# A two-layer vision transformer on one core: the V weight's and the embedding weight's way into memory at the start, the order of work at the beginning of each half of heads, and the router's place

## The reference

```python
def reference(x, ...):
    h = tok(x)                  # patches @ W_lin.T + b_lin, class token in front, + positions
    h = h + attn0(norm(h))      # 16 heads of 64; softmax(q k' / 8), causal mask, @ wo.T
    h = h + ffn0(norm(h))       # 256 -> 1024 -> 256, rounded to 1/256; gelu by 33 knots
    h = h + attn1(norm(h))      # 16 heads of 64, no mask, + bo
    return h + moe(norm(h))

def moe(x):                     # 8 experts, each 256 -> 1024 -> 256, all computed for all tokens
    logits = einsum('bld,ed->ble', x, gate_weight)
    kth = sort(logits.reshape(-1))[4 * 256 * 6 - 1]     # one threshold over all logits
    gates = logits * (logits >= kth)
    hh = gelu(einsum('bld,ehd->bleh', x, w1) + b1)
    y = einsum('bleh,edh->blde', hh, w2) + b2.T
    return einsum('blde,ble->bld', y, gates)
```

## Time and profile before

| what | value |
| --- | --- |
| median of three executions | 1000.7 us |
| the profiled execution's own time | 1000.7 us |
| its span | 998.9 us |
| TensorE, VectorE, ScalarE, GpSimd busy | 941.7, 579.5, 544.4, 154.6 us |
| 0 to 55 us (opening, first scores): TensorE busy | 41.19 us |
| 55 to 230 us (most of layer 0's attention): TensorE busy | 168.69 of 175 us |
| 230 to 345 us (its end, feed-forward): TensorE busy | 103.81 of 115 us |
| 355 to 528 us (most of layer 1's attention): TensorE busy | 166.60 of 173 us |
| 528 to 575 us (expert stage's start): TensorE busy | 37.35 of 47 us |
| 575 to 998.9 us (experts): TensorE busy | 414.60 of 423.9 us |

### The profile page before, as it was taken

The page is one execution under the profiler, slowest core; times in us unless marked ns, Lnnn a source line. Parts: engine busy times, 40 slices in busy tenths (PEclk is TensorE's granted clock), DMA queues, the critical chain, the costliest instruction groups (busy, mean ns, idle before and its releaser), DMA issues.

```text
span 998.9 us, 18661 instructions
## 1 busy us (share of the span) xinstructions
PE 941.7 (94%) x7159; PEld 870.7 (87%) x7159; DVE 579.5 (58%) x1251; ACT 544.4 (54%) x1570; POOL 154.6 (15%) x173
## 2 busy tenths in 40 slices
PE   5899999999799999999996899999999999999998
PEld 5877888888677878888886898999999999999998
DVE  5466574747899574666664486655354544544342
ACT  4466465643764664646554453756464756555452
POOL 0142122211000121222210000151011111101111
PEclk9999999999999999999999799999999999999999
DMA  7320000002000210000011011101111111100001
GB/s 277 136 76 1 1 2 2 2 1 84 3 1 1 85 43 2 1 2 1 1 43 43 1 62 67 43 1 43 43 44 43 43 43 44 43 1 1 1 14 37
DMA packets 8653, 34.48 MB, mean 35 GB/s; under 512 B 626, under 2 KB 5106, under 8 KB 5236
## 3 DMA queue, kind: packets, MB, share of 16 engines
q1 hardware_dynamic: 8564, 33.28, 9.2%
HBM read 32.06 MB, written 1.22 MB: 33 GB/s over the span
## 4 chain that ended last, share of the span: by engine, by line
issue 31%; PE 24%; POOL 5%; DVE 5%; ACT 2%; POOLq 0%; DVEq 0%; ACTq 0%
PE D L553 8%; PE O L553 7%; POOL h L348 4%; PE O L694 2%; PE T L680 2%; PE S L669 1%; DVE wslot L1094 1%; PE S L553 1%; DVE hid L1481 1%; PE S L663 1%; POOL h L360 1%; ACT hid L1066 1%; ACT work L1062 1%; PE O L799 1%; POOL vbuf L358 1%
## 5 line engine op out<-in xcount | busy, mean ns | idle before, releaser
L1481 DVE TENSOR_TENSOR hid<-work,hid 128x300 fp32r<-128x300 f32 (+1 forms) x256 | 139.3, 564 | 200.1 <-ACT hid L1066 200.0
L553 PE MATMUL O<-hid,wslot 128*128 128x300 f32 (+3 forms) x1680 | 242.4, 302 | 0.0
L553 PEld LDWEIGHTS O<-hid,wslot 128*128 128x128 f32 x1680 | 234.7, 190 | 0.6
L553 PE MATMUL D<-xn,wslot 128*128 128x300 f32 (+3 forms) x1368 | 224.4, 309 | 4.6 <-ACT work L950 2.6
L553 PEld LDWEIGHTS D<-xn,wslot 128*128 128x128 f32 x1368 | 198.8, 190 | 10.0 <-ACT work L950 2.9
L1062 ACT ACTIVATE work<-D,prm 128x300 f32<-128x300 f32 (+1 forms) x128 | 66.7, 521 | 185.6 <-PE D L553 185.5
L960 ACT ACTIVATE probs<-S,negmax 111x111 f32<-111x111 f32 (+1 forms) x352 | 117.5, 359 | 53.4 <-DVE negmax L1242 53.2
L532 POOL TENSOR_TENSOR probs<-probs,rsum 111x444 f32<-111x444 f32 (+1 forms) x88 | 80.9, 920 | 379.8 <-DVE rsum L1250 379.8
L553 PE MATMUL S<-xn,wslot 128*128 128x300 f32 (+3 forms) x864 | 137.1, 306 | 0.0
L553 PEld LDWEIGHTS S<-xn,wslot 128*128 128x128 f32 x864 | 126.4, 193 | 0.3
L1242 DVE TENSOR_REDUCE negmax<-S 111x4 f32<-111x444 f32 (+1 forms) x88 | 52.6, 600 | 72.1 <-PE S L669 72.1
(11 more groups left out here) (163 smaller groups left out, 1158.7 us busy)
## 6 DMA issues: line engine op xcount, KB each, us to landing
raw<-in_moe SPq DMA_DIRECT2D x16, 1024.0 KB, 4.8
raw<-in_attn SPq DMA_DIRECT2D x8, 1024.0 KB, 4.9
work<-in_x SPq DMA_DIRECT2D x2, 1008.0 KB, 7.9
raw<-in_ffn SPq DMA_DIRECT2D x1, 1024.0 KB, 4.7
w2f<-in_ffn SPq DMA_DIRECT2D x1, 1024.0 KB, 6.8
raw<-in_x SPq DMA_DIRECT2D x2, 504.0 KB, 5.5
out<-h SPq DMA_DIRECT2D x3, 300.0 KB, 2.7
raw<-in_w_lin SPq DMA_DIRECT2D x1, 768.0 KB, 4.1
```

The lines of the kernel that those rows point to most:

```text
L553: mm = pe.matmul(psum, a, b, start=(first and k == 0), stop=(k == 3 * n - 1))
L1481: nc.vector.tensor_tensor(moe_hid(s, 1), moe_g(s)[:, 0:w], moe_hid(s, 0).bitcast(F32), ALU.subtract).then_inc(m_hid, 1)
```

## The change

1. The raw transfer of V's weight of layer 0 goes into `w2f` and waits for nothing. The second feed-forward weight, which lands in `w2f` too, waits for V's split. The other pieces close ranks in the two raw buffers (`RING`). GpSimd's split of V waits for K's low part.
2. The embedding weight is transferred and split in two halves, interleaved with the halves of chunk 0 of x. TensorE multiplies both output halves with the first half of the rows, then both with the second.
3. The masks are cast between the two drains of chunk 1. The twelve idle matmuls go.
4. In the first round of a half the transposes of u-1 come before the scores of u on TensorE, and their copy before the row maximum on VectorE. At u = 0 the V product comes before the scores.
5. The router's chunks 0 to 2 and the last mean move to the end of `attention(1)`, into banks of their own, the last variance behind s = 0, the last normalisation ahead of the experts on ScalarE and VectorE. The last two quarters of the first expert's second weight are split behind it. Chunk 3 of the router follows s = 5. The search starts after s = 5 in place of s = 8. `gateT` is cleared whole in layer 1's fifth round, and no longer at the start of the search.

```diff
+        RING = [0, 1] + [i for i in range(FIRST_W, NPIECE) if i not in (V_ATTN0, W2_FF)]
@@ sync
+                if i == V_ATTN0:
+                    sp.dma_start(w2f[:, :], weights[i - FIRST_W]).then_inc(v0_in, 16)
+                    continue
                 if i == W2_FF:
+                    sp.wait_ge(*piece_split(V_ATTN0))
                     sp.dma_start(w2f[:, :], weights[i - FIRST_W]).then_inc(w2_in, 16)
                     continue
+                if i >= FIRST_W:
+                    sp.wait_ge(*piece_split(RING[ring(i) - 2]))
+                if i == 0:
+                    sp.dma_start(w_half(dst, 0), w_half(src, 0)).then_inc(w_in, 16)
+                    dst, src = w_half(dst, 1), w_half(src, 1)
@@ gpsimd, split
+                if i == V_ATTN0:
+                    pool.wait_ge(*piece_split(i - 1))
@@ tensor, router
+            ROUTER_BANK = [BO[0], BT[0], BS[1], BO[1]]
+            def turn_logits(c):
+                pe.wait_ge(lt_out, max(c, 1) + 1)
@@ tensor, attention
                 for i in range(8):
-                    if l == 0 and i == QH:
-                        keep_busy("qk", i, 12)
                     project_qk(i)
...
-                    if u < NUNIT:
+                    if half_begins(u):
+                        if u == 0:
+                            project_v(u)
+                        else:
+                            transposes(2 * u - 2)
                         scores(u)
-                    if 0 <= u - 1 < NUNIT:
-                        transposes(2 * u - 2)
-                    if u < NUNIT:
+                    else:
+                        if u < NUNIT:
+                            scores(u)
+                        if 0 <= u - 1 < NUNIT:
+                            transposes(2 * u - 2)
+                    if 0 < u < NUNIT:
                         project_v(u)
...
                         values(u - 1)
+                    if l == 1 and u == NUNIT + 1:
+                        router(0)
                     if due is not None:
                         project_out(due, 1)
+                    if l == 1 and u == NUNIT + 1:
+                        router(1)
+                        mean(3, 3)
+                        router(2)
@@ tensor, start
+            pe.wait_ge(w_low, 1)
+            pe.wait_ge(x0_low, 1)
+            for dc in range(KD):
+                embed_part(0, dc, range(KF // 2), True, False)
             pe.wait_ge(*piece_split(0))
-            embed(0, 0)
-            embed(0, 1)
+            pe.wait_ge(*piece_split(1))
+            for dc in range(KD):
+                embed_part(0, dc, range(KF // 2, KF), False, True)
@@ tensor, moe_up
-                    if s == 1:
-                        mean(3, 3)
-                    if s == 4:
+                    if s == 0:
                         variance(3, 3)
-                    if s in (2, 3, 5):
-                        router((2, 3, 5).index(s))
-                    if s in (5, 6, 7):
-                        turn_logits(s - 5)
-                    if s == KH:
+                    if s in (2, 3, 4):
+                        turn_logits(s - 2)
+                    if s == 5:
+                        router(3)
+                    if s == 6:
                         turn_logits(3)
@@ scalar
             square(3, 3)
+            inv_root(3, 3)
...
-                if s == 6:
-                    nc.scalar.preload_act_table_set("natural_log_exp_and_others")
-                    inv_root(3, 3)
@@ vector, prepare_gates
-                nc.vector.memset(gateR.bitcast(F32), 0.0).then_inc(params, 1)
+                nc.vector.memset(gateT[:, :].bitcast(F32), 0.0).then_inc(params, 1)
@@ vector, experts
+            finish(3, 3)
+            for k in (SPLITS - 2, SPLITS - 1):
+                low_quarter(FIRST_W + W_MOE + 1, k)
...
+                if s == 2:
+                    move_logits(3)
                 if s == 5:
-                    finish(3, 3)
-                if 4 <= s <= 7:
-                    move_logits(s - 4)
-                if s == KH:
                     start_search()
-                if m % 2 == 0 and 1 <= n <= 4:
+                if s == 6:
+                    search(0)
+                if m % 2 == 0 and 1 <= n <= 4 and s > KH:
                     search(8 * (n - 1) + m // 2)
```

More of the change, by code:

```diff
@@ L242, in ring @@
         def ring(i):
-            return i if i < 2 else i - 3 - past(i)
+            return RING.index(i)
         def piece_split(i):
@@ L412, in place_in_half, with half_begins @@
             return GROUPS[c].index(g), len(GROUPS[c])
+        def half_begins(u):
+            return u < NUNIT and place_in_half(u)[0] == 0
         def qk_blocks(u):
@@ L565, in normed, with embed_part @@
                 return [xn[:, k, kk, sl] for k in range(2)]
+            def embed_part(c, dc, ks, first, last):
+                a, w = CHUNKS[c]
+                wl = [wslot[:, WSLOTS - 1, k, 0:KF * D].rearrange("p (a n) -> p a n", n=D) for k in range(2)]
+                for i in ks:
+                    (wh, ww) = [t[:, i, dc * P:(dc + 1) * P] for t in wl]
+                    (xh, xl) = [hid[:, c % 2, k, i * w:(i + 1) * w] for k in range(2)]
+                    for a, b in ((wh, xh), (wh, xl), (ww, xh)):
+                        mm = pe.matmul(BD[dc][:, 0:w], a, b, start=first, stop=(last and i == KF - 1 and a is ww))
+                        first = False
+                if last:
+                    mm.then_inc(emb_mm, 1)
             def embed(c, dc):
-                a, w = CHUNKS[c]
                 if dc == 0:
[L571 to L579, removed]
+                    pe.wait_ge(*piece_split(1 + c))
+                pe.wait_ge(h_set, KD * (c - 1) + dc + 1)
+                embed_part(c, dc, range(KF), True, True)
             NORMED = [h_set, h_attn[0], h_ff, h_attn[1]]
@@ L611, in variance, with router @@
                 mm.then_inc(ln_var[n], 1)
+            ROUTER_BANK = [BO[0], BT[0], BS[1], BO[1]]
+            def router(c):
+                a, w = CHUNKS[c]
+                if c == 0:
+                    pe.wait_ge(params, 6)
+                pe.wait_ge(ln_out[3], c + 1)
+                split_products(pe, ROUTER_BANK[c][0:GROWS, 0:w],
+                               lambda i: [gateR[:, k, i, :] for k in range(2)],
+                               lambda i: normed(i, slice(a, a + w)), KD, lt_mm)
+            def turn_logits(c):
+                pe.wait_ge(lt_out, max(c, 1) + 1)
+                for g in GROUPS[c]:
+                    mm = pe.transpose(BT[0][0:NTOK[g], g * E:(g + 1) * E], logT[0:E, cols(g)], ident[0:E, 0:E])
+                mm.then_inc(log_mm, 1)
             def attention(l, n):
@@ L807, in _ @@
             attention(1, 2)
[L809 to L826, removed]
             def sum_counts(i):
@@ L1095, in low_quarter, with build_masks @@
                                         ALU.subtract).then_inc(dve_split if k == SPLITS - 1 else dve_part, 1)
+            def build_masks():
+                dve.wait_ge(mats_in, 64)
+                nc.vector.tensor_copy(masku[:, :], maskf[:, 2, :]).then_inc(masks, 1)
+                for l in range(2):
+                    for i in range(QH):
+                        ins = nc.vector.tensor_copy(maskb[:, l, i, :], maskf[:, l, :])
+                ins.then_inc(masks, 1)
             def set_h(c):
                 for dc in range(KD):
+                    if c == 1 and dc == 1:
+                        build_masks()
                     dve.wait_ge(emb_mm, KD * c + dc + 1)
@@ L1162, in low_x0, with low_w @@
                                         ALU.subtract).then_inc(start_split if k else x0_low, 1)
-            low_part(0)
+            def low_w(k):
+                dve.wait_ge(*((high_ready, 1) if k else (w_high, 1)))
+                high, low = piece_place(0)
+                nc.vector.tensor_tensor(w_half(low, k), w_half(piece_raw(0), k), w_half(high.bitcast(F32), k),
+                                        ALU.subtract).then_inc(start_split if k else w_low, 1)
+            low_w(0)
             low_x0(0)
+            low_w(1)
             low_x0(1)
@@ L1178, in _ @@
             low_part(2)
-            dve.wait_ge(mats_in, 64)
-            nc.vector.tensor_copy(masku[:, :], maskf[:, 2, :]).then_inc(masks, 1)
-            for l in range(2):
-                for i in range(QH):
-                    ins = nc.vector.tensor_copy(maskb[:, l, i, :], maskf[:, l, :])
-            ins.then_inc(masks, 1)
             dve.wait_ge(params, 3)
@@ L1289, in attention @@
                     due = out_due(u)
-                    if u < NUNIT:
+                    if half_begins(u):
+                        if u > 0:
+                            move_t(2 * u - 2)
                         row_max(2 * u)
-                    if 0 <= u - 1 < NUNIT:
-                        move_t(2 * u - 2)
+                    else:
+                        if u < NUNIT:
+                            row_max(2 * u)
```

(4 more changed lines are left out.)

43 lines of the change are left out of this document (26 added, 17 removed).

## The result

The changed kernel took 984.56 us (median of four; 982.26 to 987.36) against 1000.82 before. The ratio is 0.9846, interval [0.9815, 0.9877]: about 15 us faster, 16.3 by the medians. The forecast was 24.5 us faster, 976.2 us, in a range that ended at 984.5. The profiled execution took 987.36 us, with a span of 985.6 against 998.9.

The account below looks back on a forecast made before the run. TensorE, busy 94% of the span, was taken to bound the kernel. Gains of 6.3 + 6.0 + 12.2 = 24.5 us from 1000.7 gave 976.2 us, range 969.5 to 984.5.

Parts of the forecast that it names:

- Part 1: The opening: earlier first start, masks moved, V's weight without a wait; first transposes at 50.35, gain 6.3 us (4 to 7.3).
- Part 2: Half beginnings: transposes fill the wait before the scores, 0.41 us at each of 14; net gain 6.0 us (3 to 7.7).
- covered by 0.7 us: Half beginnings: a row maximum 0.53 us late ends the last exponential at 76.8, before the next scores start at 77.5.
- the 1.2 us for second transposes: Half beginnings: second transposes that waited for VectorE's copy, three of eight places, wait less; a gain of 1.2 us.
- The term of 0.45 us for layer 1's first unit: Layer 1's first unit: scores come later behind the V product, so the next scores begin 0.45 us later, a loss.
- Rival B: Opening and half beginnings: GpSimd sets the first transposes, late row maxima the next scores; low ends give 981.5 us, chance 0.16.
- the signs named for being wrong: Scores at half beginnings still wait, second scores of halves wait for exponentials, or a new stand opens before the fifth group.
- Rival D: Attention: clock closes, with fillers gone and new stands of 1.3 and 0.5 us before the first transposes; 1006 us, chance 0.03.
- Rival A: Expert stage: no second clock drop behind the second count's stand, 2.4 us less, so 973.8 us; chance 0.32.
- after 9 us at full rate: Expert stage: argument against no second clock drop, that the same stand closed the gate before, after 9 us at full rate.
- Part 3: The expert stage's start: router and normalisation work moved earlier, first count at 544.3 instead of 556.30; gain 12.2 us (9 to 13).

Follow-up runs that it names:

- old beginnings: The change with scores first again, on both engines, at all half beginnings but layer 0's first: 980.23 us, ratio 0.9792 to the kernel before.
- TensorE's new order alone: The change with VectorE's old order at half beginnings (row maximum before the copy of the first transposes), TensorE's new order kept: 978.39 us, ratio 0.9777.
- the copy first: The change with VectorE's copy of the second transposes ahead of the first reciprocal at half beginnings: 975.30 us, ratio 0.9746 to the kernel before.
- the best version: The copy first, plus layer 1's first unit in the old order and ScalarE's two expert weight copies moved behind the 16th group: 972.42 us, ratio 0.9716.

## Why the prediction was wrong

- **Part 1, +6.3 forecast, +6.2 measured.** The path was right: GpSimd ended last. V's split took 4.83 us for 4.55, which was absorbed: the output weight's copy followed the last Q/K copy and not V's split. The embedding gave 0.6 us less than written. That shift reached the first projection (34.94 for 34.4) and shrank on the way only because the forecast had sized the later steps a little long: the output weight's copy came at 43.01 for 42.7, the transposes at 50.48 for 50.35. And other profiles of the same opening gain 5.1 to 6.5 us. So the path was right, and the agreement within 0.1 us was luck.
- **Part 2, +6.0 forecast: the step that failed.** "Put ahead of the scores they fill the wait: scores start as before, and what is behind them comes 0.41 us earlier." The scores did start so. But what is behind them did not come 0.41 us earlier. The row maximum's 0.53 us was followed only to the next scores ("covered by 0.7 us"), not to the values. Values need a copy that VectorE issues behind a reciprocal, and so behind the first exponentials. Without clock falls part 2 came to -5.3 + 3.1 = -2.2 us. The experiments show it. Where VectorE comes late out of a normalisation, its old order brings the values back to 5.19 us after the scores, the kernel before's own figure, so even without the swap the 0.41 us is not gained there. The copy ahead of the reciprocal brings them to 4.54. Over the fourteen beginnings (from layer 0's third and layer 1's second score group to each layer's last) the lead fell by 1.5 us in the change (clock taken out), stayed with the old beginnings, grew by 2.6 with TensorE's new order alone, and by 5.8 with the copy first; forecast were 6.5 before the loss at layer 1's first unit. One term was also too large: of the 1.2 us for second transposes some 0.75 came with the copy first, for at three beginnings the lead grew by 0.63 us instead of 0.38. The term of 0.45 us for layer 1's first unit held: the lead went from 5.42 to 4.96.
- **Rival B** had seen that late row maxima could eat the gain, but with the next scores as the ones that wait, and with 3 us left of part 2 at the least. None of the signs named for being wrong came at the fourteen beginnings: scores wait at most 0.2 us there, the only scores that wait for exponentials are the two of the layers' second units, and no stand opened before the expert stage's fifth group. The wait that did come, at the values, had no sign in the forecast.
- **The clock.** Rival D named lapses in the attention, but for lost fillers and at the first transposes. They came behind the new stands, in some executions: 3.1 us in each of two profiles, and 1.5 us more in one of them. Part 2's stands were not foreseen, so neither were these. Rival A asked for no fall behind the second count; in this profile it came (12 matmuls in 3.35 us), in those of the new order on TensorE alone and of the copy first it did not, with the same stand of 2.21 us. The forecast's reading that the gate had closed before "after 9 us at full rate" is off: in the kernel before full rate had lasted from 555.5 to 562.3, 6.8 us, with the stand inside.
- **Part 3, +12.2 forecast, +12.3 measured.** The forecast's own terms give a first count at 544.25, so 12.05 us and not 12.2; that changes nothing. The half rate from 545 to 556 us in the kernel before is in this gain: the forecast took its paces per group at full rate, so it had this gain in its sum without naming it. TensorE worked there from 546.1 to 555.5; at full rate half of that would have done, so by this estimate some 4.7 of the 12.3 us are clock. The stand of 2.2 us stayed, as written. That it hung on ScalarE's weight copies is shown by the best version.

With -2.2 for +6.0 and one fall of 3.1 us the forecast's own sum is 976.2 + 8.2 + 3.1 = 987.5; the profiled execution took 987.36. This closes the account and proves nothing more, for the -2.2 and the 3.1 are read from that same execution.

## What to carry to other kernels

When an operation is swapped on an in-order queue, follow every later item of that queue to whoever waits for it, not only the nearest consumer. Here the item that hurt stood three places behind the delayed one, after one that waits for another engine. A wait that is filled on the bounding engine is only a gain if the next wait on that engine has slack of the same size; a table of the lead at like instructions in both traces shows within one round where it has not.

## What the runs showed of the hardware

- Stands of TensorE of 1.1 to 1.4 us among dense work were followed by 1.2 GHz in some executions and not in others: at layer 1's unit 18 in one profile, at layer 0's in another, at none in a third kernel with 1.1 us of fillers in each stand. The kernel's times fell into groups near 982 and 987 us, with mean granted clocks of 0.997 and 0.990 to 0.993; that the falls alone make the groups is not shown.
- The same stand of 2.2 us at the second count was followed by half rate in the change's profile (12 matmuls in 3.35 us) and by full rate in those of 978.46 and 974.25 us.
- A stand of 2.89 us before 40.53 us ended in half rate (granted 0.57 from 40 to 44); one of 2.61 us at the same place in the kernel before did not (1.00). One profile each.
- One and the same opening began its matmuls between 8.78 and 10.30 us in eight profiles, as the first half of x landed earlier or later (ScalarE's copy of it started between 6.35 and 7.87).
